# Decoder layer: position term moved into the causal mask, q, k and v split straight from PSUM, value bias folded at setup, new step order

## The reference, cut to what matters

```python
x = x + self_attention(layernorm(x))                     # 8 heads of 128, one head for k and v
x = x + cross_attention(layernorm(x), context, ...)      # 16 heads of 16
x = x + experts(layernorm(x))                            # 8 experts, best 2 of each row, and a shared one

# self attention
q = x @ Wq.T + sinusoidal_pe(T)      # the same pe for each head
k = x @ Wk.T + sinusoidal_pe(1)      # row 0 of the table for every key
v = x @ Wv.T
probs = softmax(where(causal, q k^T / sqrt(128), min)) ; out = (probs v) @ Wo.T

# cross attention: biases on q, k, v and on the output; scores + attn_mask + 2 * side bias + padding
out = (softmax(scores) (context @ Wv.T + bv)) @ Wo.T + bo
```

## Time and profile before

| what | number |
|---|---|
| time, median of 3 | 2268.11 us (2265.85 to 2270.7) |
| span of the profiled execution | 2269.1 us, granted TensorE clock 0.979 of full speed on the mean |
| TensorE matmuls (PE) | 2080.3 us busy, 92% of the span, 24128 instructions |
| TensorE weight loads (PEld) | 1807.7 us, 80% |
| VectorE (DVE) | 1862.2 us, 82% |
| ScalarE (ACT) | 2024.8 us, 89% |
| GpSimd (POOL) | 1781.9 us, 79% |
| transfers | 367.16 MB in 711784 packets, 162 GB/s on the mean |

### The profile page before, as it was taken

The page is one execution under the profiler, slowest core; times in us unless marked ns, Lnnn a source line. Parts: engine busy times, 40 slices in busy tenths (PEclk is TensorE's granted clock), DMA queues, the critical chain, the costliest instruction groups (busy, mean ns, idle before and its releaser), DMA issues.

```text
span 2269.1 us, 73067 instructions
## 1 busy us (share of the span) xinstructions
PE 2080.3 (92%) x24128; PEld 1807.7 (80%) x24128; DVE 1862.2 (82%) x6768; ACT 2024.8 (89%) x5937; POOL 1781.9 (79%) x1899
## 2 busy tenths in 40 slices
PE   4679999999999999999999999999999999999876
PEld 3458888888888888888888888888888888788755
DVE  4578888888888888888888888888888888888863
ACT  5589999999999998999999999999999999899862
POOL 2358888788888877888888888888888888788773
PEclk9789999999999999999999999999999999999998
DMA  4387778688777779776766887777788688788760
GB/s 144 109 182 162 164 164 174 158 170 190 169 158 164 168 155 180 175 160 160 174 167 160 188 180 161 169 164 172 155 183 182 161 160 169 150 164 186 167 135 19
DMA packets 711784, 367.16 MB, mean 162 GB/s; under 512 B 561392, under 2 KB 659952, under 8 KB 711408
## 3 DMA queue, kind: packets, MB, share of 16 engines
q1 hardware_dynamic: 711408, 362.50, 72.8%
HBM read 202.98 MB, written 25.17 MB: 101 GB/s over the span
## 4 chain that ended last, share of the span: by engine, by line
PE 57%; issue 13%; POOL 11%; ACT 8%; DMA 6%; DVE 4%; SPq 1%; ACTq 0%; POOLq 0%; DVEq 0%
PE ps_c_hidden L972 14%; PE ps_c_out L972 13%; PE ps_a_misc L972 13%; DMA b_probsT_hi_lo<-b_probs_hi_lo 5%; PE ps_b_misc L1109 5%; POOL bias L516 3%; PE ps_b_scores L1095 3%; PE ps_a_misc L1051 2%; POOL ctxT_hi L482 2%; ACT c_relu L678 2%; POOL a_qT_lo L474 2%; ACT ps_b_probs L652 2%; POOL ctxT_lo L485 2%; ACT a_qT_hi L597 2%; PE ps_a_scores L1032 1%
## 5 line engine op out<-in xcount | busy, mean ns | idle before, releaser
L516 POOL TENSOR_TENSOR bias<-bias,b_mask 128x512 f32<-128x512 f32 x512 | 644.8, 1274 | 6.2 <-DMA bias<-in_bias 5.8
L832 DVE CUSTOM_DVE_ANT_0 b_neg_scores<-ps_b_scores,bias 128x256 f32<-128x256 f32 x1024 | 391.6, 420 | 70.3 <-POOL bias L516 34.9
L839 DVE TENSOR_TENSOR b_probs_hi_lo<-ps_b_probs,b_probs_hi_lo 128x512 f16<-128x512 f32 x512 | 352.3, 688 | 106.0 <-ACT b_probs_hi_lo L660 103.6
L537 POOL TENSOR_TENSOR c_hidden_lo<-c_hidden,c_hidden_hi 128x512 f16<-128x512 f32 x288 | 335.1, 1164 | 48.4 <-issue 32.7
L972 PE MATMUL ps_c_hidden<-c_xT_hi,w_hi 128*128 128x256 f16 x1152 | 316.8, 275 | 20.2 <-ACT c_relu L678 20.2
L530 POOL TENSOR_TENSOR c_hidden<-c_relu 128x512 f32<-128x512 f32 x288 | 300.2, 1042 | 32.1 <-ACT c_relu L678 12.7
L972 PE MATMUL ps_c_out<-w_hi,c_hidden_hi 128*128 128x256 f16 x1152 | 315.3, 274 | 9.9 <-DVE acc L943 9.9
L972 PE MATMUL ps_c_hidden<-c_xT_lo,w_hi 128*128 128x256 f16 x1152 | 316.3, 275 | 0.0
L972 PE MATMUL ps_c_hidden<-c_xT_hi,w_lo 128*128 128x256 f16 x1152 | 316.3, 275 | 0.0
L972 PE MATMUL ps_c_out<-w_lo,c_hidden_hi 128*128 128x256 f16 x1152 | 315.5, 274 | 0.0
L972 PE MATMUL ps_c_out<-w_hi,c_hidden_lo 128*128 128x256 f16 x1152 | 315.4, 274 | 0.0
(11 more groups left out here) (194 smaller groups left out, 7498.1 us busy)
## 6 DMA issues: line engine op xcount, KB each, us to landing
bias<-in_bias SPq DMA_DIRECT2D x256, 512.0 KB, 4.4
q_stack<-qk_scratch SPq DMA_DIRECT2D x256, 64.0 KB, 2.6
x_ln<-in_x SPq DMA_DIRECT2D x32, 256.0 KB, 4.5
ctxT<-in_ctx SPq DMA_DIRECT2D x32, 256.0 KB, 4.5
x<-in_x SPq DMA_DIRECT2D x32, 256.0 KB, 5.3
qk_scratch<-b_qT_hi_lo SPq DMA_DIRECT2D x32, 256.0 KB, 4.6
qk_scratch<-b_kT_hi_lo SPq DMA_DIRECT2D x32, 256.0 KB, 3.8
k_stack_even<-qk_scratch SPq DMA_DIRECT2D x128, 64.0 KB, 2.5
```

The lines of the kernel that those rows point to most:

```text
L516: gp.tensor_tensor(part, part, b_mask[:, :], ALU.add).then_inc(b_c_ok, 1)
L537: gp.tensor_tensor(c_hl[:, u, :], c_h[:, :], c_hh[:, u, :], ALU.subtract).then_inc(c_h_ok, 1)
L832: last = dve.tensor_tensor_reduce(out=b_t[:, u, c, :], in0=ps_bs[:, c * T:(c + 1) * T], in1=bias[:, slot, at:at + T], scale=-2.0, scalar=3 ...
L839: dve.tensor_tensor(b_p2[:, j % DEPTH, :, 1, :], ps_bp[:, :].rearrange("p (c t) -> p c t", c=CT), b_p2[:, j % DEPTH, :, 0, :], ALU.subtrac ...
```

## The change

The position term. `a_kv` adds the row of the table to k by one more matmul (the row times ones) ahead of the product. Since (q + pe) k = q k + pe k, a new step `a_pk` forms pe k once per batch in the bank of the scores with the six matmuls of a score step; VectorE adds the constant mask to it, and the sum `a_tri` stands in place of the constant in the eight score steps.

The splits. With the addition gone, the parts of k and v are taken straight from PSUM, 512 columns at a time: `hi` by ScalarE, `lo` by VectorE; so too for each round of q and for the value rows of the cross attention. Rounds of q alternate between two banks. GpSimd loses all these steps, and gets the scaling of heads 0, 2, 4 and 6 of the self attention from ScalarE.

The value bias. bv Wo + bo is formed once (`b_c0`, at batch 0) and added to the residual in place of bo. GpSimd's setup grows from 7 to 14 counted steps.

The order. All five lists are new, and `LAGS` goes from 6 to 8. The diff, cut to its core:

```diff
+POOL_HEADS = [0, 2, 4, 6]
+ACT_HEADS = [h for h in range(AH) if h not in POOL_HEADS]
...
     sync="""
-        b_store_q:0@4 b_pT:15@5 b_store_k:0@4 b_stack_q:0@4 b_stack_k:0@4 b_pT:0@4 c_f2:8@6 b_pT:1@4 b_load:0@4
...
-        b_pT:13@4 b_pT:14@4 b_load:7@4 b_split_q:0@3""",
+        b_pT:14@7 b_store_q:0@6 b_pT:15@7 a_T:0@5 b_store_k:0@6 b_stack_q:0@6 b_stack_k:0@6 c_f2:8@8 b_load:7@7
...
+        b_load:6@6 b_pT:12@6 b_pT:13@6 b_split_q:0@5""",
     gpsimd="""
...
+        b_comb:7@4 c_f1:1@5 c_lo:1@5 c_f1:2@5 c_lo:2@5 c_f1:3@5 a_n:6@3 b_comb:8@4 b_comb:9@4 b_comb:10@4
+        b_comb:11@4 c_lo:3@5 c_f1:4@5 b_comb:12@4 c_lo:4@5""",
     scalar="""
...
+        w_split:12@1 b_o:0@2 a_n:1@0 a_pt:0@0 a_s:3@0 a_s:4@0 a_pt:1@0 a_n:3@0 a_pv:0@0 a_s:5@0 c_ln:0@2 b_s:0@1
+        c_T:0@2 b_p:0@1 w_split:13@0 a_pt:2@0 a_pv:1@0 w_split:14@0 a_s:6@0 b_s:1@1 c_gate:0@2 c_f1:0@2 b_p:1@1
...
     tensor="""
-        a_kv:0@2 b_pv:7@4 c_f2:6@5 a_q:0@2 b_pv:8@4 b_s:14@4 b_pv:9@4 b_T:0@3 a_q:1@2 b_s:15@4 b_pv:10@4 b_q:0@3
-        a_s:0@2 a_q:2@2 b_pv:11@4 b_kv:0@3 a_s:1@2 b_pv:12@4 c_f2:7@5 b_pv:13@4 a_s:2@2 a_pt:0@2 a_q:3@2 a_s:3@2
-        a_pt:1@2 b_pv:14@4 b_pv:15@4 a_pv:0@2 a_s:4@2 b_o:0@4 c_f2:8@5 a_s:5@2 b_wo:0@4 a_pv:1@2 a_pt:2@2
-        a_s:6@2 b_kv:1@3 a_s:7@2 a_pt:3@2 a_pv:2@2 c_T:0@4 b_s:0@3 a_pt:4@2 b_s:1@3 c_gate:0@4 c_f1:0@4 b_s:2@3
-        a_pv:3@2 c_f1:1@4 a_pt:5@2 b_s:3@3 c_f1:2@4 c_f2:0@4 b_s:4@3 c_f1:3@4 a_pv:4@2 c_f2:1@4 b_s:5@3 c_f1:4@4
-        a_pt:6@2 c_f2:2@4 b_s:6@3 c_f1:5@4 b_pv:0@3 b_s:7@3 b_pv:1@3 a_pv:5@2 c_f1:6@4 b_s:8@3 b_pv:2@3 c_f2:3@4
-        a_pv:6@2 a_pt:7@2 b_s:9@3 c_f1:7@4 c_f2:4@4 b_s:10@3 a_pv:7@2 b_pv:3@3 b_pv:4@3 b_pv:5@3 b_s:11@3
-        a_wo:0@2 c_f1:8@4 b_s:12@3 a_T:0@1 b_pv:6@3 c_f2:5@4 b_s:13@3""",
+        a_s:4@2 b_wo:0@4 a_pt:1@2 a_s:5@2 a_pv:0@2 b_s:0@3 a_s:6@2 b_s:1@3 c_T:0@4 a_pv:1@2 a_pt:2@2 b_s:2@3
+        c_gate:0@4 c_f1:0@4 a_pt:3@2 a_pv:2@2 c_f1:1@4 b_s:3@3 b_pv:0@3 a_s:7@2 c_f1:2@4 a_pt:4@2 c_f2:0@4
+        b_s:4@3 a_pv:3@2 c_f1:3@4 a_pt:5@2 b_s:5@3 c_f2:1@4 a_pv:4@2 b_s:6@3 c_f1:4@4 c_f2:2@4 a_pt:6@2 b_pv:1@3
+        b_s:7@3 a_pv:5@2 c_f1:5@4 b_c0:0@2 b_pv:2@3 b_s:8@3 b_pv:3@3 a_pt:7@2 b_pv:4@3 a_pv:6@2 b_s:9@3 c_f2:3@4
+        b_pv:5@3 a_pv:7@2 c_f1:6@4 b_s:10@3 b_pv:6@3 c_f2:4@4 b_s:11@3 a_wo:0@2 b_s:12@3 c_f1:7@4 a_T:0@1
+        b_pv:7@3 b_s:13@3 c_f2:5@4 a_kv:0@1 c_f1:8@4 b_pv:8@3 b_pv:9@3 b_pv:10@3 b_s:14@3 a_q:0@1 b_T:0@2
+        c_f2:6@4 a_pk:0@1 b_s:15@3 a_q:1@1 b_q:0@2 a_s:0@1 b_pv:11@3 a_q:2@1 a_s:1@1 b_kv:0@2 a_q:3@1 b_pv:12@3
+        a_s:2@1 b_pv:13@3 c_f2:7@4 b_pv:14@3 b_pv:15@3 b_kv:1@2 a_s:3@1 b_o:0@3 c_f2:8@4 a_pt:0@1""",
...
+        q_bank = [ps_am, ps_apt]
...
         # GpSimd: a_kv, a_q_lo and b_v_lo go; new:
+            def a_n(b, h):
+                u = h % DEPTH
+                gp.wait_ge(a_i_ok, after(b, AH, h + 1))
+                gp.tensor_tensor(a_p[:, u, 0:128], a_p[:, u, 0:128], a_inv[:, u, 0:1].to_broadcast([P, 128]), ALU.mult)
+                gp.tensor_tensor(a_p[:, u, 128:384], a_p[:, u, 128:384], a_inv[:, u, 1:2].to_broadcast([P, 256]),
+                                 ALU.mult).then_inc(a_np_ok, 1)
...
         # ScalarE
+                act.activation(a_kvh[:, :], ps_am[:, :], ACT.Copy, scale=1.0 / W_UP).then_inc(a_kvh_ok, 1)
...
+                act.wait_ge(a_q_ps, after(b, 4, r + 1))
                 act.wait_ge(a_s_ps, after(b, AH, 2 * r + 2 - AH))
+                act.activation(a_qh[:, 2 * r:2 * r + 2, :], q_bank[r % 2][:, :].rearrange("p (n t) -> p n t", n=2), ACT.Copy,
+                               scale=1.0 / W_UP).then_inc(a_qh_ok, 1)
...
         # VectorE
+                dve.scalar_tensor_tensor(out=a_kvl[:, :], in0=ps_am[:, :], scalar=1.0 / W_UP, in1=a_kvh[:, :],
+                                         op0=ALU.mult, op1=ALU.subtract).then_inc(a_kvl_ok, 1)
+
+            def a_pk(b, _):
+
+                dve.wait_ge(a_pk_ps, after(b, 1, 1))
+                dve.tensor_tensor(a_tri[:, :], ps_as[:, 0:384], tri, ALU.add).then_inc(a_tri_ok, 1)
...
+                dve.scalar_tensor_tensor(out=a_ql[:, 2 * r:2 * r + 2, :],
+                                         in0=q_bank[r % 2][:, :].rearrange("p (n t) -> p n t", n=2), scalar=1.0 / W_UP,
+                                         in1=a_qh[:, 2 * r:2 * r + 2, :], op0=ALU.mult,
+                                         op1=ALU.subtract).then_inc(a_ql_ok, 1)
...
         # TensorE
+                pe.matmul(ps_am[:, 0:T], pe_r[:, :], ones[:, :], start=True, stop=False)
...
+            def a_pk(b, _):
+                pe.wait_ge(a_kvl_ok, after(b, 1, 1))
+                pe.wait_ge(a_t_ok, after(b, AH, 0))
+                for out, t0, keys in [(ps_as[:, 0:128], 0, P), (ps_as[:, 128:384], P, T)]:
+                    for n, (q, k) in enumerate([(pe_h, a_kvh), (pe_h, a_kvl), (pe_l, a_kvh)]):
+                        last = pe.matmul(out, q[:, t0:t0 + P], k[:, 0:keys], start=(n == 0), stop=(n == 2))
+                last.then_inc(a_pk_ps, 1)
...
+            def b_c0(b, _):
+                if b == 0:
+                    weights(b, W10)
+                    pair_product(ps_bm[:, 0:D], lambda s, k: (bv_h if s == "h" else bv_l)[:, k, :],
+                                 lambda m, k: w(m, XO0 + k * D, D)).then_inc(b_c0_ps, 1)
```

## The result

The changed kernel takes 2318.36 us (median of 4 runs, 2311.55 to 2323.43) against 2266.98 us before on the same chip: a ratio of 1.0232, 95% interval 1.0206 to 1.0258. It is slower by 51 us, which is the side that was forecast, and inside the range (2250 to 2338); the time forecast was 2302.

The account below looks back on a forecast made before the run. TensorE's work plus its waits, 66.48 us a batch, was taken as the bound. Terms summed to +1.35, taken as 1.25 for overlap: 39 us over 31 periods, -5 from the fill, so 2302 us; range 2250 to 2338.

Parts of the forecast that it names:

- (1): From `b_wo`'s last matmul to the gate: chain of 7.3 us over 3.83 of TensorE work, wait +1.05 us a batch.
- (4): Stacks of q and k, from `b_q` to `b_s:0`: new wait of 0 to 1.5 us a batch, taken as 0.5.
- the fall of the clock: Slower rival: the longer wait before the gate halves TensorE's clock, 1.5 us a batch, 2349; two slower rivals together 0.18.
- TensorE work: New matmuls in `a_kv` (0.11) and `a_pk` (0.49) add 0.60 us a batch, hidden only if a wait shrinks.
- (2): From the gate to the first output product `c_f2:0`: wait falls from 1.23 us to 0.4, so -0.8 a batch.
- (3): Wait for the last transposed tile of a batch, `b_pT:15`: 0.3 us for 0.63, so -0.3 a batch.
- (5): GpSimd's four mask adds stand ahead of `c_lo:3`, needed by `c_f2:3`: 0 to 1.5 us a batch, taken as 0.3.
- the gain in the fill: First batch loses GpSimd's hop in q rounds, gets weight splits ahead of its keys: -12 to +6 us, taken as -5.
- still 7 to 7.6: Sign of being right: `b_wo`'s last matmul to the gate still takes 7 to 7.6 us with less work in it.
- a waiting `b_s:0` of over 1 us: Sign of being wrong: TensorE waits over 1 us at `b_s:0`, the first score step of the cross attention.
- None of the three is the bound: ScalarE (about -3.4 us a batch), GpSimd (-1.7), VectorE (about even): their relief counts only where TensorE waits for them.

Follow-up runs that it names:

- the filler: The changed kernel with 22 matmuls of ones, results unused, put into TensorE's wait ahead of `b_s:0`: 2304.2 us, 1.0170 to the kernel before.

## Why the prediction came out as it did

The side was right, and so was the size of the term that the forecast put first, (1). The time was 16 us short, since (4) was sized too small; within it lies the fall of the clock, which the sum counted at nothing. Term by term, per batch:

| step | forecast | measured | from |
|---|---|---|---|
| TensorE work | +0.60 | about +0.5 | usual spacing of every kind of matmul, summed over a batch, about 61.8 to 62.3 |
| (1) `b_wo` to gate, alone | +1.05 | +1.07 | 7.29 with the stacks in time, less the 3.83 of work: 3.46 |
| (4) `b_s:0` waits for the stacks | +0.5 | +1.31 | 8.60 less 7.29 |
| (2) gate to `c_f2:0` | -0.8 | -0.75 | 6.84 - 5.61 = 1.23 to 6.98 - 6.50 = 0.48 |
| (3) transposed tiles | -0.3 | -0.3 | 12.6 to 6.4 us in 20 batches |
| (5) `c_lo:3` on GpSimd | +0.3 | -0.1 | output products behind their usual spacing, 0.15 to 0.08; before, no wait for them is listed |
| sum | +1.35 | +1.73 | period: +1.60 |

Without (4) the measured terms come to +0.42 a batch, 13 us, and the gain in the fill takes 8 of them. The two runs in which the wait at `b_s:0` is mostly gone stand at 8 and 11 us over the kernel before (1.0036 and 1.0048). So most of what makes the change slower is the term that the forecast held for small, and that the time fell into the range owes something to errors that offset one another: (4), with the clock in it, was put too low, and (5), the work on TensorE and the time of the fill too high.

**(1) was right, and could be read only once (4) was out of the way.** The chain was given 7.3 us; in the three runs in which the stacks come about 2 us earlier it takes 7.29, 7.29 and 7.32. In the changed kernel itself the stretch is 8.60, which by the prediction's own list counts as a miss ("still 7 to 7.6").

**(4) is the term that failed, in size.** The prediction said that 20.0 us of way stood against some 15 us of work, took 17.5 as covered "with the waits of (3), and as far as (1) allows", and 1 to 2 us as saved. The way is 18.4 us, as guessed. The cover is not: the waits of (1) lie behind `b_s:0` in the new list, not ahead of it, and can't cover it, and those of (3) had just been reckoned away. TensorE is there some 16.1 us behind `b_q`, which leaves a wait of 2.35 (44.7 in 19 batches; 2.94 in the batch shown). The prediction named the sign that would prove it wrong (a waiting `b_s:0` of over 1 us), and it came. That four loads decide 44 us was not seen either: the sixteen issues were counted as one block, though the earlier trace rows gives 3.65 us for eight.

**The clock was a rival and is a term.** It was priced at 1.5 us a batch and given a small chance since the wait of (1) was cut up by small steps. The wait of (4) is not cut up: 2.94 us with two matmuls, and then 0.65 for 4.82 us. It came in 14 of some 20 batches and costs about 0.45 us a batch, a third of the price, perhaps (this was not tested) since much of the half-speed stretch lies where TensorE would have waited for `c_T` and the gate anyway. At least part of the 0.45 lies in the 1.31 above, not on top of it: with the filler `b_wo` to the gate takes 8.42 in place of 8.60. The Trainium skill, "TensorE: Matmul & The Clock Gate", part 1, says that idle time brings the clock to half; by that this rival was likely, and the trace agrees on the fall, with 0.65 behind the wait.

**The three other engines.** Their busy times moved about as forecast (ScalarE 59.7 us a period, the mean of six, GpSimd's head scaling 0.40 + 0.61 = 1.0 us against 1.2 taken):

```profile
L487 POOL TENSOR_TENSOR a_probs<-a_probs,a_inv 128x256 f32<-128x256 f32 x128 | 78.5, 614 | 0.0
...
L486 POOL TENSOR_TENSOR a_probs<-a_probs,a_inv 128x128 f32<-128x128 f32 x128 | 51.2, 400 | 40.0 <-DVE a_inv L798 40.0
```

"None of the three is the bound" was too short a sentence. Undone alone, the scaling on GpSimd is worth 105 us in the new lists, and the second bank 138. Each is part of what lets the new lists run with few waits, and neither shows in a busy share. GpSimd, busy 74%, is the better place for the scaling by 105 us than ScalarE as tried, although its 256 columns cost 614 ns against ScalarE's 502 in the earlier trace rows. The Trainium skill, "GPSIMD Engine Reference", section 4.1, sends elementwise work to VectorE; no run here tests that for the scaling.

**Fill and rest.** The fill gave 7.9 us where 5 were taken. GpSimd was not late at `c_lo:3`. The forecast's +39 for 31 periods and -5 for the fill stand against +49.6 and -7.9 in the profiled execution.

Open: how the 11 us between the profiled execution's difference of span and that of the medians are spread, what `a_pk` costs to better than 9 us, and what the new order itself is worth.

## What to carry to other kernels

Ask of each wait which work stands ahead of it on that engine, and count as cover only that: a wait that comes later in the list covers nothing. Where a step waits for a block of transfers, count the issues on the queue and ask which of them its first instruction reads; a wait that stands for more than it reads cost 42 us here and one semaphore took it back. A part that looks worthless by busy shares can be what the order rests on: undo the parts one at a time before calling any of them free.

## What the runs showed of the hardware

Work that nobody needs made the kernel faster: 22 matmuls a batch inside a wait of 3 us kept the granted clock at 1.00 in place of 0.65 behind it, worth some 14 us. For the small loads on SyncE's queue the count weighs more than the bytes: the eight of q's stack, 64 KB each, took 3.81 us of issuing in the batch shown (0.48 each), one load of 256 KB 0.57 and one store of 256 KB 0.38. GpSimd multiplies by a broadcast column at 614 ns for 256 columns, less than the 731 ns of its plain add in the earlier trace rows.
